# GpSimd forms the scan's drive with time on the partitions, TensorE turns it back into PSUM, and a third fold moves to GpSimd

## The reference

```python
x = x + tanh(g_xattn) * ssm(ctx, layernorm(x))
x = x + tanh(g_ffn) * ffn(layernorm(x))

# ssm: u = silu(conv(in_proj(ctx))), delta = softplus(dt_proj(dt_lo)), A = -exp(A_log)
def step(state, xs):
    d_t, B_t, C_t, u_t = xs
    dA = exp(d_t[..., None] * A)
    state = state * dA + (d_t * u_t)[..., None] * B_t[:, None, :]
    y_t = einsum('ben,bn->be', state, C_t)
# y = (y + D * u) * silu(z)

# ffn: gate = bitlinear(x, w_gate); up = bitlinear(x, w_up)
# return bitlinear(fwht(silu(gate) * up), w_down)
```

## Time and profile before

| | |
|---|---|
| Median of three runs | 283.89 us (280.01 to 284.46) |
| Profiled execution | 282.87 us, of which 280.7 us is the span of the trace |
| TensorE busy, weight loads busy | 186.5 us, 145.5 us |
| VectorE busy | 235.6 us (84%) |
| ScalarE busy | 163.5 us (58%) |
| GpSimd busy | 194.4 us (69%) |

### The profile page before, as it was taken

How to read it: one execution, slowest core, us unless ns; L and a number is a source line. 1 busy time by engine, 2 the same in 40 slices (tenths; PEclk the granted TensorE clock), 3 DMA queues, 4 the chain that set the end, 5 groups by cost and what they waited for, 6 DMA issues and landing times. The chain is left out here.

```text
span 280.7 us, 3113 instructions
## 1 busy us (share of the span) xinstructions
PE 186.5 (66%) x982; PEld 145.5 (52%) x988; DVE 235.6 (84%) x320; ACT 163.5 (58%) x286; POOL 194.4 (69%) x137
## 2 busy tenths in 40 slices
PE   4477665770865668686794939468678495695683
PEld 2344345560654457455593827357566275572662
DVE  4389999989989999478979996986999996558974
ACT  1487959922943993897089586834474541624131
POOL 1100794697997389999999999999996609305700
PEclk9999959596578556975579797955978889979599
DMA  2990000000000000000000000000000000000001
GB/s 57 290 358 15 2 0 2 0 0 0 0 2 1 0 0 0 4 0 0 1 0 0 2 0 21 0 19 1 0 0 2 20 0 21 0 0 0 19 21 37
DMA packets 8145, 6.29 MB, mean 22 GB/s; under 512 B 2202, under 2 KB 7874, under 8 KB 8130
## 3 DMA queue, kind: packets, MB, share of 16 engines
q1 hardware_dynamic: 7154, 6.02, 6.6%
q10 hardware_dynamic: 976, 0.09, 0.3%
HBM read 5.05 MB, written 1.05 MB: 22 GB/s over the span
## 5 line engine op out<-in xcount | busy, mean ns | idle before, releaser
L985 POOL TENSOR_TENSOR drive<-du,Bs 128x512 f32<-128x512 f32 x60 | 105.5, 1783 | 35.5 <-ACT Bs L732 34.1
L1115 DVE TENSOR_TENSOR_SCAN state<-decay,drive 128x1024 f32<-128x1024 f32 x32 | 87.8, 2744 | 15.7 <-issue 13.3
L742 ACT ACTIVATE decay<-delta,zero_c,aneg 128x255 f32<-128x255 f32 x128 | 66.4, 593 | 9.9 <-DVE delta L1139 9.9
L394 PE MATMUL PY<-id,prod 128*128 128x128 f32 x256 | 48.1, 351 | 1.4 <-DVE prod L1157 1.4
L394 PEld LDWEIGHTS PY<-id,prod 128*128 128x128 f32 x256 | 43.1, 188 | 2.8 <-DVE prod L1157 1.6
L1157 DVE TENSOR_TENSOR prod<-state,BC 128x1024 f32<-128x1024 f32 x32 | 38.5, 1202 | 0.1
L378 PE MATMUL BC<-bc,sel 96*128 96x256 bf16 x64 | 16.1, 345 | 27.2 <-DVE prod L1157 27.2
L837 ACT COPY hT<-GP 128x1024 f32<-128x1024 f32 x8 | 8.1, 1007 | 36.5 <-PE GP L521 36.5
L378 PEld LDWEIGHTS BC<-bc,sel 96*128 96x128 bf16 x64 | 6.0, 110 | 36.1 <-issue 34.2
L732 ACT COPY Bs<-BC 128x512 f32<-128x512 f32 x32 | 18.4, 576 | 9.4 <-PE BC L365 9.3
L1011 POOL TENSOR_TENSOR wnat<-wnat 128x512 f32<-128x512 f32 x12 | 23.2, 1931 | 0.0
(11 more groups left out here) (185 smaller groups left out, 388.9 us busy)
## 6 DMA issues: line engine op xcount, KB each, us to landing
wnat<-in_L_ffn_w_gate_dram SPq DMA_DIRECT2D x1, 1024.0 KB, 9.9
xs<-in_x_dram SPq DMA_DIRECT2D x1, 1024.0 KB, 12.3
wnat<-in_L_ffn_w_up_dram SPq DMA_DIRECT2D x1, 1024.0 KB, 12.4
wnat<-in_L_ffn_w_down_dram SPq DMA_DIRECT2D x1, 1024.0 KB, 11.3
out_dram<-ot SPq DMA_DIRECT2D x8, 128.0 KB, 1.7
ctxs<-in_ctx_dram SPq DMA_DIRECT2D x1, 384.0 KB, 7.4
ctxs<-in_ctx_dram SPq DMA_DIRECT2D x1, 128.0 KB, 2.7
inw<-n_L_xattn_in_proj_w_dram SPq DMA_DIRECT2D x1, 128.0 KB, 2.7
```

The costliest lines, as they stand in the source:

```text
L394: last = nc.tensor.matmul(PY[:, E * c + P * h:E * c + P * (h + 1)], prod[:, g % RING, h, n, P * c:P * (c + 1)], id32[:], is_transpose=True ...
L742: last = nc.scalar.activation(decay[:, m % RING, h, n, 1:L], delta[:, b % 2, h, 1:L], ACT.Exp, bias=zero_c[:], scale=aneg[:, h, NB * j + n ...
L985: last = nc.gpsimd.tensor_tensor(drive[:, m % RING, h], du[:, b % 2, h, :].unsqueeze(1).to_broadcast([P, NB, L]), Bs[:, m % RING], ALU.mult)
L1115: nc.vector.tensor_tensor_scan(state[:, g % STATES].rearrange("p h n l -> p (h n l)"), decay[:, g % RING].rearrange("p h n l -> p (h n l)" ...
```

## The change

1. **The drive's layout.** GpSimd now makes the drive with time on the partitions: `driveT[time, c, n, channel] = duT[time, c, channel] * BT[time, c, n]`. B is now one number per partition, so the instruction is a `tensor_scalar` of 256 elements, four to a step, in place of two `tensor_tensor` of 512. `duT` is made once a batch by four transposes (`du_T`) and a ScalarE copy (`copy_duT`); `BT` comes out of `x_dbl` by four more small matmuls and a 32-element copy (`copy_BT`). `B_rows` and `copy_B` stay for the first two steps alone.
2. **Turned back by TensorE.** `drive_rows(m, h)` turns the four 128x128 blocks of one half into the PSUM bank PB. The bank holds one half only, so the next half's transposes wait for the scan that reads this one.
3. **The scan in two halves**, each over 512 elements, with the drive read from PSUM. `times_C` now stands between the two halves of the next step's scan. TensorE's `accumulate` is cut in two as well, and the two `drive_rows` calls are put ahead of its halves.
4. **A third fold.** `fold_tile` makes all three butterfly stages on GpSimd; `hadamard_mm` is then eight 128x128 products for every batch (with `had`), and `build_hadamard` is gone.
5. **Other calls are moved.** On TensorE all feed-forward and front calls now stand behind the step's two `accumulate` halves, several in one place. `gate_times_up` stands one place earlier on VectorE (ahead of step 6's scan calls for tile 0), and `delta_on_vector(1)` stands ahead of step 4's. `softplus` and `dt_proj` of batches 2 and 3 move to the next batch's step 0.

```diff
-            def accumulate(g):
+            def accumulate(g, h):
...
+            def drive_rows(m, h):
+
+                pe.wait_ge(pool_drive, drives_before(m + 1))
+                if m > DVE_DRIVES or h > 0:
+                    pe.wait_ge(dve_scan, HALF * m + h)
+                else:
+                    pe.wait_ge(act_B, DVE_DRIVES)
+                for n in range(NB):
+                    for c in range(LC):
+                        last = nc.tensor.transpose(PB[:, L * n + P * c:L * n + P * (c + 1)],
+                                                   driveT[:, m % RING, c, n, P * h:P * (h + 1)], id32[:])
+                last.then_inc(pe_drive, 1)
...
+                for c in range(LC):
+                    for h in range(HALF):
+                        last = nc.tensor.matmul(BT_part(n)[:, DS * c:DS * (c + 1)], u[:, n % 3, h, P * c:P * (c + 1)],
+                                                xpwT[:, h, 0:DS], start=(h == 0), stop=(h == HALF - 1))
...
-                    if f < B - 1:
-                        last = nc.tensor.matmul(dst[:, E * (a // 2):E * (a // 2 + 1)], hT[:, t, a, :],
-                                                had2[:, a % 2].rearrange("p i c -> p (i c)"),
-                                                start=(a % 2 == 0), stop=(a % 2 == 1))
...
+                    last = nc.tensor.matmul(dst[:, P * a:P * (a + 1)], hT[:, t, a, :], had[:], start=True, stop=True)
...
+                    if DVE_DRIVES <= g + 1 < B * STEPS:
+                        drive_rows(g + 1, 1)
+                    if g + 1 < B * STEPS:
+                        C_rows(g + 1)
+                    accumulate(g, 0)
+                    if DVE_DRIVES <= g + 2 < B * STEPS:
+                        drive_rows(g + 2, 0)
+                    accumulate(g, 1)
...
-                for h in range(HALF):
-                    last = nc.gpsimd.tensor_tensor(
-                        drive[:, m % RING, h], du[:, b % 2, h, :].unsqueeze(1).to_broadcast([P, NB, L]),
-                        Bs[:, m % RING], ALU.mult)
+                pool.wait_ge(act_BT, b + 1)
+                pool.wait_ge(act_duT, b + 1)
+                if m >= RING + DVE_DRIVES:
+                    pool.wait_ge(pe_drive, HALF * drives_before(m - RING + 1))
+                for c in range(LC):
+                    for n in range(NB):
+                        last = nc.gpsimd.tensor_scalar(driveT[:, m % RING, c, n], duT[:, b % 2, c],
+                                                       BT[:, b % 2, c, NB * j + n:NB * j + n + 1], 1.0, ALU.mult, ALU.mult)
...
-                    scan(g + 1)
+                        scan(g + 1, 0)
+                    times_C(g)
+                    if g + 1 < B * STEPS:
+                        scan(g + 1, 1)
```

More of the change, by code:

```diff
@@ L406, in accumulate @@
+                if j == STEPS - 1 and h == HALF - 1:
+                    pe.wait_ge(pool_diag, 1)
+                    for e in range(HALF):
+                        for c in range(LC):
+                            last = nc.tensor.matmul(PY[:, E * c + P * e:E * c + P * (e + 1)],
+                                                    u[:, b % 3, e, P * c:P * (c + 1)], diag[:, e],
+                                                    start=False, stop=(e == HALF - 1 and c == LC - 1),
                                                     skip_group_check=True)
@@ L608, in _ @@
             B_rows(1)
-            in_proj(1, [0])
-            B_rows(2)
-            in_proj(1, [1])
+            du_T(0)
             C_rows(0)
-            for m in range(3, AHEAD):
-                B_rows(m)
+            in_proj(1)
             for k in range(B):
@@ L627, in _ @@
                             tokens_T(f)
+                        if old:
+                            down(p, 0)
+                        if front:
+                            in_proj(n)
+                    if s == 4:
+                        if k == 0:
+                            weight_T(0)
+                            weight_T(1)
+                        if 1 <= k < B - 1:
+                            du_T(k + 1)
+                        if new:
+                            gate(f, 0)
+                            gate(f, 1)
+                        if old:
+                            q2_T(p, 1)
                     if s == 5:
+                        if k == 0:
+                            du_T(1)
+                            weight_T(2)
+                            weight_T(3)
                         if new:
-                            gate(f, 1)
+                            up(f, 0)
+                            up(f, 1)
+                        if front:
+                            x_dbl(n)
                     if s == 6:
@@ L1328, in _ @@
             first_drive(0)
-            scan(0)
+            scan(0, 0)
+            scan(0, 1)
             first_drive(1)
@@ L1350, in _ @@
                     if s == 6:
+                        if new:
+                            gate_times_up(f, 0)
                         if old:
```

234 lines of the change are left out of this document (108 added, 126 removed).

## The result

The changed kernel takes 292.7 us (median; 291.3 to 293.8) against 283.7 us for the kernel before: a ratio of 1.036, 95% interval 1.031 to 1.041. It is slower, where I had forecast 282 us and no change. The time lies inside the stated range (271 to 298), on the side of the rival whose clock stays low.

The account below looks back on a forecast made before the run. VectorE was taken as the bound, it and GpSimd holding each other up. A stretch of 199.5 us, 2.0 above before, less 2.1 in the tail, put on 282.87, gave 282.8, stated as 282 us; range 271 to 298.

Parts of the forecast that it names:

- the rival whose clock stays low: TensorE's clock stays low half of the time, as before: stretch 215.7 us, 299 in all; decides from 30% low; chance 0.22.
- tail: After the last product: hadamard_mm(2, 1) gets shorter, so gate can start sooner; at most 2.1 us won.
- scans and products: VectorE's two half scans and a product take 3.6 us a step, 111.6 us in all, for 119.9 before.
- I take 15% low: TensorE's clock in the stretch is low 15% of the time, adding 0.15 x 49 to 192.2 us: 199.5.
- handoffs: VectorE waits after a half scan while TensorE turns four blocks: 3.3 us at the high clock, 6.5 at the low.
- bursts: TensorE's other calls between accumulate and the next drive_rows overrun what VectorE covers: 10.8 us high clock, 46.8 low.
- new waits: VectorE's other calls wait at gate_times_up, residual's chain, weight_out, round_down, tokens_out: 11.5 us high clock, 21.3 low.
- all 20 us of before: VectorE's idle time in the stretch before the change, mainly ahead of scans; all of it was to go.
- my sign for "right": A granted TensorE clock of 0.85 to 0.95 in the stretch would show the forecast right.
- GpSimd being held four times a step: Rival: GpSimd's four drive instructions are still held, 6.1 us a step, over 320 us in all; chance 0.04.
- PSUM's cost: Rival: PSUM as source costs each half scan 0.065 us or more, 3.9 us, so 286 or more; chance 0.04.
- a bound for the scans: Scans at their lower bound, with the clock always high, take the whole from 275.5 to 271 us.

Follow-up runs that it names:

- the kernel with the first move: Changed kernel with drive_rows(g+2, 0) put ahead of accumulate(g, 0) in the first step of batches 1 to 3; ratio 1.018.
- The last kernel above: Changed kernel with drive_rows and hadamard_mm(tile 0) ahead of accumulate at batch starts, weight_scale(2) ahead of drives(8), up(tile 0) earlier in step 5; 276.0 us, ratio 0.974.

## Why the prediction was wrong, point by point

The sum was made against the profiled execution: 199.5 us for the stretch, 2.1 less in the tail. The terms:

| term | forecast, us | measured, us |
|---|---|---|
| scans and products | 111.6 | 111.1 |
| VectorE's other calls | 55 | 54.9 |
| idle, if all were at the high level / at the low one | 25.6 / 74.6 | mixed |
| share of the time at the low level | 15% | 30% (clock 0.85) |
| idle in the stretch | 32.9 | 42.9 |
| the stretch | 199.5 | 208.85 |
| up to product 0 | 0 | -0.8 |
| tail | -2.1 | +0.8 |

- **GpSimd and the scans** were right to 0.5 us: no long cases, 0.55 us an instruction, 1.215 us a half, GpSimd off the scans' path. That the PSUM source costs nothing was right too: the one half scan of the stretch with its drive in SBUF took 1229 ns, the 60 from PSUM 1215 in the mean. The rule of the Trainium skill, VectorE: DVE Perf Modes, section on the TRN2 errata, by which PSUM adds to the fixed part, disagrees with these two rows; the measurement decides.
- **The step that failed is "I take 15% low".** A mean clock of 0.85 is 30% of the time at 1.2 GHz. With 30% my own sum gives 192.2 + 0.30 x 49 = 206.9 us, 2 from the measured 208.85. That nearness is partly luck: idle time is 10 us over the forecast's 32.9, and by my sorting of the waits below the terms that depend on the clock make 4.5 of them (handoffs 1.7, bursts 1.2, new waits 1.6). The other 5.4 or so had no term: the wait of 3.2 us that I missed, and 2.2 of small waits and gaps, because I let all 20 us of before go, with some 1.7 of such gaps in them. At 30% low the bursts should have been 21.6 us and were 17.4. My argument was that saturated pieces raise the clock and TensorE's idle pieces shrink. The clock did rise, 0.76 to 0.85, but TensorE's idle time in the stretch went only from 63.4 to 59.2 us, and the new order made long pieces of its own, 3.39 and 6.39 us in `accumulate` at the starts of batches 1 and 2, which lie right ahead of the bursts of `dt_proj` and `hadamard_mm`. A mean over the stretch also hides that the low level meets the pieces that VectorE waits for. I had even named 30% as the point from which the slower rival decides, and my sign for "right" (0.85 to 0.95) began at that same point.
- **The tail** was the same step once more. `gate` came 1.5 us sooner, of the 2.1 at most that I gave it; what followed took 2.3 us more than before, 1.7 of them in the last two `down`, at the low level. The same tail with the clock at 0.88, in the kernel with the first move, took 44.7 us, 1.3 under before.
- **New waits of VectorE's calls**: `gate_times_up` 6.5 us (6.3), the chain behind `residual` 2.5 (0.6 to 3.3), `weight_out` 2.8 (2.3), `round_down` 1.7 (1.8), `tokens_out` 1.1 (0.5 to 1.0). Sized well, but **one was missing**: `weight_round(2)`, 3.2 us, because `weight_scale(2)` stands on GpSimd behind `drives(8)`, whose wait for ScalarE's `copy_duT` the change added. And as prices they were misread: moving `gate_times_up` brought back 5.8 of 6.5 us before the scans, moving `up` took the wait off.
- **Bare handoffs and bursts**: about 5.5 us and 17.4 us by my sorting of the trace's waits (3.3 and 10.8 forecast at the high level, 6.5 and 46.8 at the low; 3.8 and 16.2 at 15% low). A bare handoff took 0.87 us at the high level, for 0.78.
- **The third fold** costs nothing in sum, as forecast, but not because it is hidden: it held up `split` ahead of `residual` by 2.6 us and shortened `hadamard_mm` by about as much.
- **The rivals**: the clock rival was the one that came, though at 30% and not at half; GpSimd being held four times a step did not come, nor did PSUM's cost. The range's lower end of 271 us rests on a bound for the scans that my sum nowhere gives.

What stays open: how much of the 24.6 us of turning is clock and how much is TensorE's plain time. No run holds the clock fixed. That the share of 15% failed is read from the granted clock; what it cost is my sum's figure. The last kernel above speaks for the place of the work over the mean clock: at 0.88 its stretch took 189.5 us, less than my sum gave for a clock that is always high (192.2).

## What to carry to other kernels

When a change puts an engine between a producer and the bounding engine through one buffer, everything else in that engine's queue is priced too: list what stands between two handoffs, and look for a wait for the bounding engine itself ahead of them. To take a wait off, move the work that is late into the engine's idle piece; moving the call that waits mostly renames the wait. And a gain in TensorE's time is only as good as the clock at that place, so read the clock where VectorE waits, not as a mean.

## What the hardware showed that I had not expected

- GpSimd's one-input `tensor_scalar` (128x256) took 551 ns beside scans with one SBUF operand, 702 beside half scans with two, and 787 beside 1024-element scans with two; `zn`'s long cases (1532 ns median), the same form, are not typical of it.
- The holding goes the other way too, for short calls: `split`'s 32x256 call with two SBUF inputs took 0.41 us three times and 3.02 us the one time that two of GpSimd's folds ran beside it.
- With more TensorE work the granted clock was higher (0.91 for 0.85 with the transposes doubled); 240 more transposes, 26 us of TensorE's time at the high level, cost 12 us.
